# Folding keys before projecting values in the opening of a one-core graph-attention kernel

## The reference

```python
h = jnp.maximum(_layernorm(x, axis=-1), 0.0)        # x: (4096, 512)
q = h @ W_q.T + b_q;  k = h @ W_k.T + b_k;  v = h @ W_v.T + b_v
z = (1.0 / math.sqrt(512)) * (q @ k.T)              # (4096, 4096)
spare_z = z * adj                                   # adj: 0 or 1
spare_z = jnp.where(spare_z == 0.0, -10000.0, spare_z)
out = jax.nn.softmax(spare_z, axis=1) @ v
return x + jax.nn.relu(out)
```

## Time and profile before

| | |
|---|---|
| median of 3 runs | 1481.22 us (1480.55 to 1481.66) |
| profiled execution, its own time | 1482.13 us |
| its span | 1480.3 us |
| PE, DVE, ACT busy | 1461.4, 1301.0, 868.7 us |
| mean granted clock of PE | 0.997 |

### The profile page before, as it was taken

The page is one execution under the profiler, slowest core; times in us unless marked ns, Lnnn a source line. Parts: engine busy times, 40 slices in busy tenths (PEclk is TensorE's granted clock), DMA queues, the critical chain, the costliest instruction groups (busy, mean ns, idle before and its releaser), DMA issues.

```text
span 1480.3 us, 24626 instructions
## 1 busy us (share of the span) xinstructions
PE 1461.4 (99%) x9414; PEld 927.0 (63%) x9414; DVE 1301.0 (88%) x1595; ACT 868.7 (59%) x1398; POOL 44.7 (3%) x27
## 2 busy tenths in 40 slices
PE   8999999999999999999999999999999999999998
PEld 4556665666666666666666666666666666666443
DVE  6877887898999999898989899989999899988985
ACT  3666665765666556655656565655665566555541
POOL 0000000000001000100010000000010001000100
PEclk9999999999999999999999999999999999999999
DMA  5445534465555665566655565656566555664252
GB/s 206 153 171 211 187 141 178 172 233 212 228 200 217 227 242 213 195 244 221 228 210 219 221 237 213 233 220 221 213 242 227 219 199 213 227 221 181 91 169 87
DMA packets 75045, 301.24 MB, mean 203 GB/s; under 512 B 8496, under 2 KB 8496, under 8 KB 73136
## 3 DMA queue, kind: packets, MB, share of 16 engines
q1 hardware_dynamic: 74928, 299.66, 54.3%
HBM read 260.84 MB, written 38.80 MB: 202 GB/s over the span
## 4 chain that ended last, share of the span: by engine, by line
PE 94%; DVE 3%; ACT 1%; issue 1%; DMA 0%; SPq 0%; POOL 0%; DVEq 0%; ACTq 0%
PE o L604 44%; PE za L552 22%; PE zd L552 11%; PE zb L552 5%; PE o L525 5%; PE o L539 4%; PE o L507 1%; PE za L613 0%; PE o L623 0%; DVE g_buf L1090 0%; DMA slots<-in_L_gnn_W_k 0%; DVE slots L1206 0%; ACT g_buf L740 0%; PE zb L613 0%; DVE slots L1177 0%
## 5 line engine op out<-in xcount | busy, mean ns | idle before, releaser
L604 PE MATMUL o<-v_buf,p_buf 128*128 128x512 f16 x3072 | 734.2, 379 | 0.8 <-DVE p_buf L1213 0.6
L604 PEld LDWEIGHTS o<-v_buf,p_buf 128*128 128x128 f16 x3072 | 300.5, 98 | 270.8 <-issue 1.5
L552 PE MATMUL za<-h_buf,g_buf 128*128 128x256 f16 x2952 | 402.2, 273 | 5.2 <-DVE g_buf L1090 2.2
L552 PEld LDWEIGHTS za<-h_buf,g_buf 128*128 128x128 f16 x2952 | 287.5, 98 | 143.3 <-ACT mm_tmp L767 3.6
L552 PE MATMUL zd<-h_buf,g_buf 128*128 128x256 f16 x1476 | 201.3, 273 | 0.0
L806 ACT ACTIVATE slots<-slots,log_p 128x1024 f32<-128x1024 f32 x128 | 146.0, 1141 | 56.6 <-DVE slots L1206 56.6
L1206 DVE TENSOR_TENSOR slots<-slots,floor_b 128x1024 f32<-128x1024 f32 x128 | 170.0, 1330 | 0.3 <-POOL floor_b L480 0.3
L1213 DVE TENSOR_TENSOR p_buf<-slots,p_buf 128x1024 f16<-128x1024 f32 x128 | 157.4, 1230 | 13.7 <-PE o L604 13.4
L1169 DVE TENSOR_TENSOR slots<-um_tmp,dm_tmp 128x512 f32<-128x512 f32 x128 | 89.2, 697 | 82.3 <-ACT dm_tmp L794 82.3
L801 ACT ACTIVATE slots<-za,c_all,kappa 128x256 f32<-128x256 f32 x128 | 72.3, 565 | 143.1 <-PE za L552 142.1
L1181 DVE SCALAR_TENSOR_TENSOR slots<-slots 128x1024 f32<-128x1024 f32 x128 | 156.0, 1219 | 0.2
(11 more groups left out here) (141 smaller groups left out, 1127.4 us busy)
## 6 DMA issues: line engine op xcount, KB each, us to landing
g_buf<-g_dram SPq DMA_DIRECT2D x108, 896.0 KB, 5.2
v_buf<-v_dram SPq DMA_DIRECT2D x128, 512.0 KB, 3.3
adj_own<-in_adj SPq DMA_DIRECT2D x92, 512.0 KB, 6.1
spare<-in_adj SPq DMA_DIRECT2D x36, 512.0 KB, 6.2
g_dram<-g_buf SPq DMA_DIRECT2D x12, 896.0 KB, 4.4
v_dram<-v_buf SPq DMA_DIRECT2D x16, 512.0 KB, 5.4
spare<-in_x SPq DMA_DIRECT2D x15, 512.0 KB, 8.1
h_buf<-h_dram SPq DMA_DIRECT2D x7, 1024.0 KB, 9.1
```

Source lines behind the costliest of these rows:

```text
L552: mm = pe.matmul(bank[:, 0:QH], g_of(i)[:, a, op, j, :], right[b][j], start=(fresh and j == 0 and m == 0), stop=(j == 1 and m == 2), skip_ ...
L604: mm = pe.matmul(o_bank[t][:, :], a[:, kt, span], v_buf[:, n % V_BUFS, kt, b, :], start=(j == 0 and kt == 0 and m == 0), stop=(j == PAIRS ...
```

## The change

On PE, in each part that has both, the chunk of keys is projected in the middle, where the values were, and the values last, where the chunk was. On ACT `copy_g` and `high_v` change places in the same way. The splitting of folded keys moves: `combine_g`, `high_g` and `low_g` of chunks 0 and 1 from the third part (i = 2) into the second (i = 1), those of chunks 2 and 3 from the first part of the next quad (i = 0) into the fourth (i = 3). On ACT `high_g` now stands ahead of `high_h`; on DVE `low_g` stands behind `low_h`, and `low_v` goes from the front part of the row to its very end.

```diff
@@ PE
-                if v_tile(k) >= 0:
+                if 1 <= g <= QUADS:
+                    project_g(g - 1, i)
+                elif v_tile(k) >= 0:
                     project_v(v_tile(k))
-                elif 1 <= g <= QUADS:
-                    project_g(g - 1, i)
...
                 if v_tile(k) >= 0 and 1 <= g <= QUADS:
-                    project_g(g - 1, i)
+                    project_v(v_tile(k))
@@ ACT
-                between = v_tile(k) < 0
-                if between or k == LATE:
-                    if i == 2:
-                        high_g(g - 1, 0)
-                    if i == 0:
-                        high_g(g - 2, 1)
-                if between:
+                if 1 <= g <= QUADS:
                     copy_g(g - 1, i)
-                else:
+                elif v_tile(k) >= 0:
                     high_v(v_tile(k))
...
-                if not between and k < LATE:
-                    if i == 2 and g >= 1:
-                        high_g(g - 1, 0)
-                    if i == 0 and g >= 2:
-                        high_g(g - 2, 1)
+                if i % 2 == 1 and 1 <= g <= QUADS:
+                    high_g(g - 1, i // 2)
                 if g + 1 < QUADS:
                     high_h(k + QUAD)
...
-                if not between and 1 <= g <= QUADS:
-                    copy_g(g - 1, i)
+                if v_tile(k) >= 0 and 1 <= g <= QUADS:
+                    high_v(v_tile(k))
@@ DVE
-                if i == 2 and 1 <= g <= QUADS:
-                    combine_g(g - 1, 0)
-                if i == 0 and 2 <= g <= QUADS + 1:
-                    combine_g(g - 2, 1)
+                if i % 2 == 1 and 1 <= g <= QUADS:
+                    combine_g(g - 1, i // 2)
                 if k == LATE:
                     add_c11(half)
-                if QUAD <= k < LATE and v_tile(k) >= 0:
-                    low_v(v_tile(k))
-                if i == 2 and 1 <= g <= QUADS:
-                    low_g(g - 1, 0)
-                if i == 0 and 2 <= g <= QUADS + 1:
-                    low_g(g - 2, 1)
                 if g + 1 < QUADS:
                     low_h(k + QUAD)
+                if i % 2 == 1 and 1 <= g <= QUADS:
+                    low_g(g - 1, i // 2)
...
                 if i == 3 and g + 1 < QUADS:
                     key_terms(g + 1)
+                if QUAD <= k < LATE and v_tile(k) >= 0:
+                    low_v(v_tile(k))
```

## The result

The changed kernel takes 1533.11 us (median of 5 runs, 1531.42 to 1535.81) against 1481.51 before: a ratio of 1.0349, interval 1.0337 to 1.0361. The forecast was 1517.3, at most 1528. The direction was right, the size was not: 51.6 us instead of 36.1.

The account below looks back on a forecast made before the run. PE, busy 99% of the span (DVE 88%), was taken as the bound; 9.0 (parts 4 to 8) + 28.4 (odd parts) - 1.3 (parts 28 to 37) = 36.1 on 1482.13 gave 1518.2, as median 1517.3 us; range 1507 to 1528.

Parts of the forecast that it names:

- The odd parts: Parts 9 to 27: `low_v`, last in DVE's row, stalls PE 1.93 us, or 4.71 with statistics; together 28.4 us.
- the even row: DVE's even parts: 3.5 us of work, ending by 17.6 or 20.4, so no lateness is carried over.
- Parts 4 to 8: Early opening: value tiles wait for DVE, so part 9 begins at 86.6, 9.0 us later.
- The clock: PE's granted clock: no fall taken behind the new stalls; each fall would cost 2 to 3 us.
- that early one: Early PE wait of 4.15 us in the kernel before, after which eight matmuls took 6.41 us instead of 3.44.
- Rival 1: PE's clock falls at the three long stalls and once in parts 4 to 8: 1526 us, chance 0.15.
- Parts 28 to 37: End of the opening: earlier splitting frees PE waits, DVE brings some new ones; a gain of 1.3 us.
- Main loop: After the opening: moved stores, loads and other waits cost nothing, 0 us.
- Rival 2: ACT's copies don't hold DVE up, so its row is shorter by its idle 2.3 us: 1493 us, chance 0.09.
- Rival 3: Not slower: DVE finishes `low_v` by 13.08 us in every row: 1480 us, chance 0.06.

Follow-up runs that it names:

- e1: The changed kernel with the statistics of a quad behind `low_v` on DVE instead of ahead of it: 1514.4 us.
- e2: The changed kernel with `low_v` of odd parts (but part 7) directly behind `low_g` on DVE: 1494.9 us.
- e3: The changed kernel with `high_h` ahead of `high_g` on ACT: 1497.2 us.
- e4: The changed kernel with 105 added matmuls of zeros on PE where it stalls, in parts 6 to 28: 1519.3 us.
- e5: The changed kernel with parts 4 to 7 in the order of the kernel before, the changed order from part 8 on: 1522.8 us.
- e6: The changed kernel with the splitting of folded keys back in the third part and the first part of the next quad, as before: 1496.3 us.
- e7: The changed kernel with the changed order only from part 28 on, earlier parts as before: 1482.4 us.
- e10: Changed order only from part 12, `high_h` ahead of `high_g`, odd parts' `low_v` behind `low_g`, next block's query combinations in parts 29, 30, 32, 34: 1480.2 us.

## Why the prediction failed in its size

- **The odd parts: right.** Forecast were stalls of 1.93 and 4.71 in 15.16 and 17.94 us from a part's start; part 14's value tile began 17.95 after part 13 (144.14 - 126.19). The waits are listed as 4.56 and 1.77 because the profile models a matmul's end 0.16 late. Sum of the ten waits in parts 10 to 28: 26.9, with 0.16 each 28.5; forecast 28.4. e1, e2 and e3 each took away one part of the row (the statistics, all that stood between `low_g` and `low_v`, the hole), and the waits of 4.56 became 1.8, 0.5 and 2.63. One slip: the even row is called 3.5 us of DVE's work; the prediction's own units give 2.7, with which its 17.6 and 20.4 are worked out, and the row took 2.8 (143.91 to 146.67).
- **Parts 4 to 8: right but for the clock.** Forecast 9.0; measured 12.0, of which 1.69 and 1.29 are two slow value tiles (4.44 and 4.04 against 2.75). In e4, where they ran at full clock, part 9 began at 85.17: the forecast's 86.6, less the 1.4 us by which that execution's value tiles began sooner.
- **The clock: the step that failed.** The sum puts it at nothing: "I take no fall, as PE had done little before that early one and is busy before these". Seven value tiles ran behind a fall: 4.44, 4.04, 4.44, 4.99, 5.21, 5.28, 4.44 us against 2.75, in sum 13.6 us, and e4 gave back 13.8. Being busy before did not help: ahead of each of the five in parts 10 to 28 TensorE had run for 15 us or more without a wait. The prediction's own list has five waits above 2 us there (2.43, three of 4.71, 2.36), and each was followed by a fall. Rival 1 had the mechanism, at 15%, but named only the three waits of 4.71 and one in parts 4 to 8, since I had let the one early example (4.15 us) stand for the shortest wait that counts; its sum then prices three falls and leaves the fourth out. Its price of 2 to 3 us a fall was somewhat high: 1.3 to 2.5.
In the openings of all the kernels, from 30 us on, a wait of up to 1.8 us was followed by slow matmuls only in part 8, where one of 3.49 or 4.32 stood just before it; each wait of 3.9 or more was. From 2.1 to 3.5 us it went either way: slow behind 2.95, 2.29 and 2.21 in the changed kernel, 2.10 in e2, 2.20 in e5 and one of three of 2.63 in e3, at full clock behind 3.36 in e6, 2.29 in e5, 2.20 in e1, the other two in e3 and 2.19 in part 4 of the changed kernel. What decides it there no run shows. The falls belonged in the sum with their odds, and in the range in full: five between parts 9 and 28 alone, at the prediction's 2 to 3 us each, are 10 to 15 us.
The Trainium skill ("TensorE: Matmul & The Clock Gate", Part 1) has the throttled state as the default that activity lifts; e4 agrees, as the clock stayed at 1.00 when zeros were multiplied in the waits.
- **Parts 28 to 37: right** (-0.9 against -1.3). The wait of 1.56 before part 34 was foreseen as 1.0 to 1.6; the other, foreseen as 0.5 in part 32, came as 0.51 within part 34. **Main loop: wrong by 1.8 us**: forecast 0. DVE left the opening later against PE than before (its `low_v` of part 36 began 2.17 us after the start of part 37, at 332.25; before 0.30, at 281.50), ACT's copies of scores waited for it, and PE waited 1.76 us for them behind part 37. e7, with the change from part 28 on alone, has the same wait.
- **Rival 2** (the row shorter by its hole) had nearly the right price for the waits: e3 is that row, made by moving one operation, with three waits of 2.63 where the rival has 2.4. As a forecast it was wrong, since the hole was there. **Rival 3** needed `low_v` by 13.08; e10 shows what comes then: no difference.
- The sum: 36.1 + 13.6 (clock) + 1.8 (behind part 37) + 0.4 (parts 29 to 36) - 1.1 (a sooner start in this execution) = 50.8, against spans 50.7 apart.

## What to carry to other kernels

When a bound engine waits in many places, work each wait out from the rows, and then price every wait of more than about 2 us on TensorE a second time, for the clock: here that second price was 13.6 us on top of some 37 us of waits. An operation that frees the only buffer of the next step belongs as far forward in its engine's row as its input allows; moving `low_v` forward in the odd parts was worth 38 us. When work moves from one row to the next, count both rows, not their sum: the total of DVE's work was unchanged, and the row that came to hold 12 us of work and two waits (of 2.64 and 2.33 us, part 13) set the pace.

## What the runs showed of the hardware

The granted clock can fall with a wait of 2.1 us (e2) and stay up with one of 3.4 (e6); equal waits of 2.63 us in one execution went either way (e3). A fall cost 1.3 to 2.5 us in the block of twelve matmuls behind the wait; in some cases the next matmuls were slow too, by up to 0.4 us (e1, a product of 1.24 us instead of 0.82). Multiplying zeros into a bank that is free keeps the clock up, and made a kernel 13.8 us faster by adding instructions (e4), though not faster than one that has no waits to fill. Replaying three in-order engines from start-to-start times met each wait between parts 9 and 28 to 0.1 us, once 0.16 is added to the listed waits.
